# A transformer and state-space kernel on one core: the slot tables of the middle phase renumbered, and its slot-count constant renamed to one that the last phase also reads

## The reference, cut to what matters

```
h = silu(conv(x @ in_proj_w));  dlt, Bm, Cm = split(h @ x_proj_w)
delta = softplus(dlt @ dt_proj_w + b);  deltaA = exp(delta * A)
for t in tokens:                       # d_state = 16, d_inner = 256
    state = deltaA[t] * state + delta[t] * h[t] * Bm[t]
    y[t]  = sum over the 16 states of state * Cm[t]
out = (y + h * D) * silu(res) @ out_proj_w
```

## Time and profile before

| | |
|---|---|
| median of three runs | 4853.02 us |
| time of the profiled execution | 4849.57 us |
| its span in the trace | 4847.7 us |
| busy PE, DVE, ACT, POOL | 4224.2, 3951.5, 3757.1, 3498.7 us |
| phase B, about | 505 to 4125 us |
| phase C, about | 4125 to 4847 us |

### The profile page before, as it was taken

One profiled execution on the slowest core, in us unless ns is written; L12 is line 12 of the kernel. 1 busy time (PEld: TensorE's weight loads), 2 busy tenths in 40 slices (PEclk: granted clock), 3 DMA queues, 4 the chain that ended last, 5 costly groups with the idle time before them and its releaser, 6 DMA issues. The chain is left out here.

```text
span 4847.7 us, 130869 instructions
## 1 busy us (share of the span) xinstructions
PE 4224.2 (87%) x45166; PEld 3208.1 (66%) x45166; DVE 3951.5 (82%) x6890; ACT 3757.1 (78%) x11543; POOL 3498.7 (72%) x2504
## 2 busy tenths in 40 slices
PE   6988699988999899998989988999899998688887
PEld 3555477776777677776777767777677776355553
DVE  4776798888888788888889878888788885588887
ACT  2555588888888788887888878888788887677774
POOL 0100798988888888987889978898798985354444
PEclk9999899999999999999999999999999999788888
DMA  1000111111111111111111111111111110000000
GB/s 26 6 5 2 53 50 38 44 38 51 52 44 38 50 45 51 40 44 44 45 52 44 38 44 52 46 44 44 44 46 44 44 44 25 5 4 3 3 3 5
DMA packets 118636, 169.33 MB, mean 35 GB/s; under 512 B 26564, under 2 KB 44423, under 8 KB 118023
## 3 DMA queue, kind: packets, MB, share of 16 engines
q1 hardware_dynamic: 109246, 160.92, 12.5%
q10 hardware_dynamic: 8776, 0.45, 0.1%
HBM read 20.79 MB, written 2.10 MB: 5 GB/s over the span
## 5 line engine op out<-in xcount | busy, mean ns | idle before, releaser
L1375 POOL TENSOR_TENSOR b_w<-b_w,b_vt 128x512 f32<-128x512 f32 x768 | 1159.2, 1517 | 350.6 <-DVE b_ss L1291 188.5
L1379 POOL TENSOR_TENSOR b_rn<-b_ssm,all_neg_half 128x16 f32<-128x16 f32 x384 | 1220.1, 3177 | 32.0
L1174 ACT ACTIVATE b_Pr<-ps,b_nm 128x96 f32<-128x96 f32 x3072 | 1002.0, 352 | 0.6
L1174 ACT ACTIVATION_READ_ACCUMULATOR b_Pr<-ps,b_nm 128x1 f32 x3072 | 673.6, 219 | 0.0
L1060 PE MATMUL ps<-b_Whi,b_xlo 128*128 128x512 f32 x1152 | 555.3, 482 | 87.8 <-ACT b_Vraw L1197 36.7
L1287 DVE TENSOR_TENSOR b_w<-ps,until_b_rotab 128x512 f32<-128x512 f32 x768 | 525.1, 684 | 112.2 <-ACT b_sq L1193 110.6
L989 PE MATMUL ps<-all_ident,b_w 128*128 128x128 f32 x3072 | 453.6, 281 | 126.5 <-ACT b_qkT L1144 90.6
L1026 PE MATMUL ps<-all_ident,b_Pr 128*96 128x128 f32 x3072 | 474.8, 278 | 99.8 <-DVE b_Pr L1338 57.0
L1193 ACT ACTIVATE b_sq<-ps 128x512 f32<-128x512 f32 x768 | 448.0, 621 | 100.4 <-PE ps L1062 93.5
L1289 DVE TENSOR_TENSOR b_vt<-ps,until_b_rotab 128x512 f32<-128x512 f32 x768 | 523.3, 681 | 0.0
L1291 DVE TENSOR_REDUCE b_ss<-b_sq 128x8 f32<-128x512 f32 x768 | 519.7, 677 | 0.0
(11 more groups left out here) (259 smaller groups left out, 9581.8 us busy)
## 6 DMA issues: line engine op xcount, KB each, us to landing
b_V<-b_Vraw SPq DMA_DIRECT2D x384, 192.0 KB, 2.6
b_V<-b_Vraw SPq DMA_DIRECT2D x384, 128.0 KB, 2.3
b_V<-b_Vraw SPq DMA_DIRECT2D x192, 64.0 KB, 2.2
b_Wraw<-in_L_ffn_Wqkv SPq DMA_DIRECT2D x36, 256.0 KB, 3.0
b_Wo<-in_L_ffn_Wo SPq DMA_DIRECT2D x6, 512.0 KB, 4.3
a_xtok<-in_L_attn_hidden_states SPq DMA_DIRECT2D x16, 128.0 KB, 2.1
out<-c_xout SPq DMA_DIRECT2D x16, 128.0 KB, 1.8
b_W<-in_L_ffn_W SPq DMA_DIRECT2D x6, 341.0 KB, 3.3
```

Source lines behind the costliest of these rows:

```text
L1174: last = nc.scalar.activation(s.Pr[:, r % 2, j, i], ps[:, S_BANK[j], i * KEYS:(i + 1) * KEYS], ACT.Exp, bias=s.nm[:, r, j, i:i + 1], accum ...
L1375: nc.gpsimd.tensor_tensor(rows, rows, s.vt[:, i % 4], ALU.add).then_inc(s.pool_add, 1)
L1379: nc.gpsimd.tensor_tensor(s.rn[:, j], s.ssm[:, j], g.neg_half[:, 0:HB], ALU.pow).then_inc(s.pool_r, 1)
```

## The change

It renumbers the slot tables of phase B, and renames its slot count. All of phase C's code and tables are left as they are.

```diff
-STEP_SLOTS = 32
-ROUND = STEP_SLOTS // ROUNDS
+SLOTS = 32
+ROUND = SLOTS // ROUNDS
...
-LATE_SLOT = {3: (0, 3), 4: (0, 1), 7: (1, 3), 8: (1, 1)}
-WO_SLOT = (12, 13)
-W1_SLOT = {5: 0, 14: 2, 18: 1}
+LATE_SLOT = {0: (0, 3), 4: (0, 1), 6: (1, 3), 7: (1, 1)}
+WO_SLOT = (11, 12)
+W1_SLOT = {5: 0, 17: 2, 21: 1}
...
-SCORE_LAG, EXP_LAG, SCALE_LAG, TURN_LAG, VALUE_LAG, COPY_LAG = 0, (3, 4), 8, (10, 12), 16, 16
-
-RES_SLOT, STATS_SLOT, END_SLOT, SPLIT_SLOT = 12, 23, 28, 7
+SCORE_LAG, EXP_LAG, SCALE_LAG, TURN_LAG, VALUE_LAG, COPY_LAG = 0, (4, 5), 8, (8, 11), 14, 15
+
+RES_SLOT, STATS_SLOT, END_SLOT, SPLIT_SLOT = 14, 24, 31, 8
...
-GELU_SLOT, RSTD_SLOT, GATE_SLOT = 20, 22, 18
+GELU_SLOT, RSTD_SLOT, GATE_SLOT = 21, 23, 19
...
-    for slot in range(STEP_SLOTS):
+    for slot in range(SLOTS):
```

More of the change, by code:

```diff
@@ L711 @@
 HALF = INNER // 2
-STEP_SLOTS = 32
-ROUND = STEP_SLOTS // ROUNDS
-QK_SLOT = {0: (0, 0), 2: (0, 2), 6: (1, 0), 7: (1, 2), 16: (0, 1), 17: (0, 3), 23: (1, 1), 24: (1, 3)}
-V_SLOT = {15: (0, 4), 20: (1, 4), 28: (0, 5), 31: (1, 5)}
-ROTATE_LAG, ADD_LAG = 2, 0
+SLOTS = 32
+ROUND = SLOTS // ROUNDS
+QK_SLOT = {0: (0, 0), 2: (0, 2), 6: (1, 0), 8: (1, 2), 16: (0, 1), 17: (0, 3), 22: (1, 1), 24: (1, 3)}
+V_SLOT = {15: (0, 4), 21: (1, 4), 29: (0, 5), 30: (1, 5)}
+ROTATE_LAG, ADD_LAG = 2, 2
 CHUNKS = (0, 2, 4, 1, 5, 3)
 CONVERT_SLOT = {0: (0, 1), 4: (2,), 8: (3,), 10: (4,), 12: (5,)}
-LATE_SLOT = {3: (0, 3), 4: (0, 1), 7: (1, 3), 8: (1, 1)}
-WO_SLOT = (12, 13)
-W1_SLOT = {5: 0, 14: 2, 18: 1}
-XT_SLOT, XN_SLOT, W2_SLOT = 22, 30, 29
-TRANSPOSE_SLOT = {21: (1, 2), 24: (1, 0), 25: (0, 2), 27: (0, 0)}
-READ_LAG = 0
-SCORE_LAG, EXP_LAG, SCALE_LAG, TURN_LAG, VALUE_LAG, COPY_LAG = 0, (3, 4), 8, (10, 12), 16, 16
-RES_SLOT, STATS_SLOT, END_SLOT, SPLIT_SLOT = 12, 23, 28, 7
-DVE_NORM_SLOT = {28: 2}
-DVE_LATE_NORM_SLOT = {5: 3}
-POOL_NORM_SLOT = {5: 0, 14: 1}
-GELU_SLOT, RSTD_SLOT, GATE_SLOT = 20, 22, 18
+LATE_SLOT = {0: (0, 3), 4: (0, 1), 6: (1, 3), 7: (1, 1)}
+WO_SLOT = (11, 12)
+W1_SLOT = {5: 0, 17: 2, 21: 1}
+XT_SLOT, XN_SLOT, W2_SLOT = 21, 31, 29
+TRANSPOSE_SLOT = {22: (0, 0), 26: (1, 2), 27: (1, 0), 28: (0, 2)}
+READ_LAG = 0
+SCORE_LAG, EXP_LAG, SCALE_LAG, TURN_LAG, VALUE_LAG, COPY_LAG = 0, (4, 5), 8, (8, 11), 14, 15
+RES_SLOT, STATS_SLOT, END_SLOT, SPLIT_SLOT = 14, 24, 31, 8
+DVE_NORM_SLOT = {27: 2}
+DVE_LATE_NORM_SLOT = {4: 3}
+POOL_NORM_SLOT = {7: 0, 16: 1}
+GELU_SLOT, RSTD_SLOT, GATE_SLOT = 21, 23, 19
 def piece_slots():
```

## The result

The changed kernel takes 4918.61 us, median of four runs (4916.99 to 4921.62), against 4851.3 us of the kernel before: ratio 1.0138, 95% interval 1.012 to 1.0155. It is 67 us slower; 4983 had been forecast, with a range of 4895 to 5055. The profiled execution took 4923.65 us, its span is 4921.7.

A forecast was written before the change was run, and what follows sets the result against it. Phase B was taken as bound by a ring of four nearly full engines, phase C by DVE; 4849.6 + 108 (phase C) + 24 (phase B) = 4981.6, 4985 on the median, written as 4983 us, range 4895 to 5055.

The forecast's parts named there:

- 108 us of four sums ahead of the spread: Phase C step end: sums 4 to 7 delay the next B spreads by 7.2 us at each of 15 boundaries.
- the return of nothing: Phase C: the step gives back none of the added 7.2 us; bounds 0 and 3.09 us, its largest gap.
- Rival 4: Phase C: the rename has no effect or DVE hides it, leaving only phase B, 4874 us; chance 0.04.
- rival 3: Phase C: PE's low clock lasts until the spread of C, costing 165 us, 5147 us; or ends earlier, 4936; chance 0.05.
- the term of +24 us: Phase B: the renumbered tables cost 0.5 us more a pair, over 48 pairs.
- that is given back: Phase B: the scale's 1.6 us gain is lost to DVE's 1.3 us wait, with maximum and rotations 1.3 us later.
- Zero, for the copy, the values and the turns: Phase B: moving copy and values earlier and turns behind the scores leaves the second square's time unchanged within some tenths.
- the ring: Phase B: PE, POOL, ACT and DVE, all nearly full, wait on each other, instead of one engine bounding it.
- The range of -72 to +96 us for phase B: Phase B: the tables change each pair by -1.5 to +2 us.
- my case: Phase C slower by 62 to 111 us, phase B within -72 and +96: 4900 to 5055 us; chance 0.73.
- Rival 1: Phase B: the earlier scale wins up to 3.6 us a pair, 173 us, more than phase C loses: 4785 us; chance 0.09.
- Rival 2: Phase B: turns behind the scores wait for each scale, 3 us a pair, 144 us: 5102 us; chance 0.09.

The follow-up runs named there:

- E2: The kernel before with the rename alone (slot count 32 also goes to phase C, phase B tables stay): 4956.81 us, ratio 1.0223.
- E3: The kernel before with two of the four sums (4 and 5) moved ahead of the next item's B spreads: 4904.30 us, ratio 1.0116.
- E1: The changed kernel without its rename: new phase B tables, phase C on its own 16 slots: 4814.90 us, ratio 0.9930 to the kernel before.
- E5: The kernel before with only the split of the input one slot later, behind DVE's reciprocal and scale: 4827.30 us, ratio 0.9957.
- E6: New tables without the rename, with the split put back ahead of the scale: 4864.41 us, ratio 1.0033 to the kernel before.
- E7 to E11: New lags on kernel before: 5176.09 us. New tables without rename, putting back all lags: 5139.35; values and copy: 4989.23; turns: 4967.58; feed-forward pieces, GELU, gate: 4968.41.

## Why the prediction was right, and the step that was wrong

**Phase C: right in its place and mechanism; the size came out by two errors that cancel.** The term was 108 us of four sums ahead of the spread. E2 measures 109, E3 57 for half of it; the new wait of 6.75 us, the distance of the first scans (47.8 us) and the unchanged gap at L1526 are as forecast, and so is the return of nothing. But a boundary costs 6.8 us and not 7.2, since the group of five sums takes 8.85 us where sum 3 alone took 1.98, so that the four add 6.87. The 5 us that this leaves over the 15 boundaries are made up at the end of the phase, by the last boundary (9.4 us) and the last item (2.8 us), which the prediction did not price. That 108 was hit so closely is luck. ACT's wait for the delta projection fell from 5.82 us to 5.09, less than the 2 us forecast, and nobody gained by it. Rival 4 (no effect of the rename) fell with E2.

**The clock: rival 3 did not come in the steady steps, though its cause did.** The low stretch doubled, as the Trainium skill in "TensorE: Matmul & The Clock Gate", Part 1, makes one expect of more idle time (by that rule, the trace agrees). It cost nothing because all of the added slow time lies in the first half of the step, where PE waits anyway: the B spread at 4586.40 waits 4.74 us for ACT's copy. What had to stay fast is the work behind the return, and the return did not move against the scan. In the last boundary it did, and 1.7 of the 2.6 us that this boundary costs above the others are the slower group of sums; of the 165 us that rival 3 priced, the rows show no more.

**Phase B: the term of +24 us had the wrong sign; it is -30 us in the trace, -33 us in E1.** The step that failed is "that is given back". The prediction let the scale come 1.6 us earlier and took it back with 1.3 us of DVE waiting and a maximum and two rotations 1.3 us later. The wait came. The maximum came no later in the step below. What was priced wrong is the split itself. The timeline of the odd step before, DVE and POOL:

```profile
2057.07 1.22 DVE L1298 TENSOR_TENSOR b_w<-b_w,b_rn 128x1024 f32<-128x1024 f32 x1
2057.23 2.19 POOL L1375 TENSOR_TENSOR b_w<-b_w,b_vt 128x512 f32<-128x512 f32 x1 [0.49 <-DVE b_ss L1291]
2058.20 1.37 DVE L1240 TENSOR_SCALAR b_xhi<-all_xT 64x256 fp32r<-64x256 f32 x1
...
2060.79 0.20 DVE L1334 RECIPROCAL b_rinv<-b_ssum 128x8 f32<-128x8 f32 x1
...
2061.90 0.95 DVE L1344 TENSOR_REDUCE b_nm<-ps 128x8 f32<-128x768 f32 x1
```

and the same place after:

```profile
2047.89 1.21 DVE L1298 TENSOR_TENSOR b_w<-b_w,b_rn 128x1024 f32<-128x1024 f32 x1
2048.05 2.18 POOL L1375 TENSOR_TENSOR b_w<-b_w,b_vt 128x512 f32<-128x512 f32 x1 [0.48 <-DVE b_ss L1291]
2050.04 0.20 DVE L1334 RECIPROCAL b_rinv<-b_ssum 128x8 f32<-128x8 f32 x1 [0.94 <-ACT b_Pr L1174]
...
2051.16 0.30 DVE L1240 TENSOR_SCALAR b_xhi<-all_xT 64x256 fp32r<-64x256 f32 x1
...
2052.68 0.96 DVE L1344 TENSOR_REDUCE b_nm<-ps 128x8 f32<-128x768 f32 x1
```

Before, the first instruction of the split takes 1.37 us and ends at 2059.57, right behind POOL's addition (2057.23 + 2.19 = 2059.42). After, it takes 0.30 us, with POOL's addition over since 2050.23. Over the whole program, before and after:

```profile
L1240 DVE TENSOR_SCALAR b_xhi<-all_xT 64x256 fp32r<-64x256 f32 x97 | 130.2, 1342 | 0.2 <-DVEq L1232 0.2
```
```profile
L1240 DVE TENSOR_SCALAR b_xhi<-all_xT 64x256 fp32r<-64x256 f32 x97 | 30.4, 313 | 0.2 <-DVEq L1232 0.2
```

One us in each "busy" duration was waiting: before, 95 of the 97 instructions start while a POOL addition (L1375) is under way and end 0.14 to 0.16 us behind its end; the others last 0.27 to 0.29 us. DVE's 0.94 us of wait for the exponentials took the place of this hidden wait and was free: from the start of the normalisation to the maximum it is 4.83 us before (2061.90 - 2057.07) and 4.79 after (2052.68 - 2047.89), not 1.3 more. The scale's start went from 3.96 us behind that same point (2061.03) to 2.39 (2050.28), and nothing was given for it. The Trainium skill, in "SBUF — State Buffer", "Who interferes with whom", gives a reason that fits: VectorE and GpSimd share a pair of ports under an exclusive lock, and an instruction that needs the pair blocks until the other engine's is done. The trace agrees in the order of ends (0.14 to 0.16 us); no run here tested that rule by itself.

In E5, where ACT's order is unchanged, the part that remains is seen alone. POOL's product from its even to its odd step comes 35.01 us later (2040.97 to 2075.98) instead of 35.65 (2044.78 to 2080.43), and its wait for the GELU falls from 0.91 us to:

```profile
2075.98 1.82 POOL L1385 TENSOR_TENSOR b_ha<-b_ha,b_hgate 128x768 f32<-128x768 f32 x1 [0.24 <-ACT b_hgate L1220]
```

**"One pair times 48" was the second error.** The distances between the POOL products (L1385) of two odd steps, worked out from their starts, are not all alike. Every eighth pair converts the next weights. In us, the means of each kind; "rest" is what is left at both ends of the phase:

```
                    30 ordinary pairs   5 converting pairs   the 10 behind them   rest     sum
before              72.02 each          89.7 each            72.3, 74.7           101.3    3445
after               71.64               84.3                 72.2, 76.7           100.0    3415
E5, split alone     71.64               89.0                 71.3, 74.6           101.3    3425
E6, all but split   72.72               84.7                 72.7, 77.3            99.0    3454
```

Of the 30 us, 11 are in the ordinary pairs (30 x 0.38) and 18 in and behind the five conversions, a place at which the prediction did not look. E5 shows what the split brings alone, 11 us in the ordinary pairs and 9 in and behind the conversions. The other tables alone (E6) gain 10 us in the second part and cost 0.7 us in each ordinary pair, 21 us; together with the split that cost is gone, and no run shows why. Which of their numbers speeds the conversion is open too; DVE's wait for ACT's converted weights fell from 62.1 to 42.7 us in all, and no run singled it out.

**Zero, for the copy, the values and the turns, held only with all the other places moved along.** The prediction priced each move against the rest of the old order. E7 to E11 show that no move can be priced so: with the lags alone the ring costs 328 us, and taking back the values, the turns or the GELU costs 148 to 169 us each. Everything but the split costs 16 us (E6), so it is near to zero only as a whole. The range of -72 to +96 us for phase B held the result because all the moves came together, not because each was small; that is luck. (The lower end of the range of "my case", 4900, does not follow from its bounds either: 4849.6 + 62 - 72 is 4840.) Rival 1 named the right mechanism, the earlier scale, and decided from 2.3 us a pair; the pass was worth 1.1 us a pair in the new tables (72.72 - 71.62, E6 against E1) and 0.4 in the old. Rival 2, paying turns behind the scores, came in part: ACT waits 244.2 us in all for PE's turns where it was 26.3. But its wait for the values, 222.0 us before, is down to 15.6 in exchange, and the piece reads wait less:

```profile
DVE b_rinv L1334 <- ACT b_Pr L1174: 288.4, 233, 2.6
ACT b_PT L1216 <- PE ps L1026: 244.2, 248, 3.2
...
ACT b_hgate L1163 <- PE ps L1118: 30.1, 99, 4.0
```
```profile
ACT b_oT L1204 <- PE ps L1041: 222.0, 273, 2.9
ACT b_hgate L1163 <- PE ps L1118: 143.0, 188, 6.2
DVE b_rinv L1334 <- ACT b_Pr L1174: 85.6, 143, 1.7
```

(after first, then before). DVE's wait for the exponentials more than tripled in a phase that got shorter.

The sum: 108 forecast and 104 to 109 measured for C, +24 forecast and -30 to -33 measured for B; 4983 - 57 = 4926, and 4919 was measured. The forecast stood because the term that was wrong in sign was small beside the other.

## What to carry to other kernels

Work put ahead of the instruction that an idle-free engine waits for costs its whole duration, straight in its amount; price it by that, price the ends of a phase apart, and check what stood beside it. Before a busy duration is used as a price, compare it with the shortest of its kind: one that is long only where it ends just behind another engine's instruction holds a wait, and a wait that replaces it is free. In a ring of engines that are all nearly full, a set of moves made together can't be priced move by move; and a phase is not one period times a count when some periods do other work.

## What the runs showed of the hardware

- The VectorE instruction of L1240 (64x256, f32 into fp32r, both in SBUF) lasts 0.27 to 0.31 us, or 1.36 when it starts behind a GpSimd addition that is under way, which was so in 95 of 97 cases; 100 us of DVE's "busy" time before was this. In E5, with the reciprocal and the scale in its place, the scale takes it in part (1.80 us instead of 0.96 at 2054.56), and POOL's clamp behind it lasts 1.10 instead of 0.29 us.
- PE's clock was at 1.2 GHz for 20 instead of 10 us of a step, and the step paid nothing for it: PE had no late work there. Only in the last boundary, low again for 3.4 us within a group of 20 sums, did the group take 10.55 us instead of 8.85.
